# The output offset of the attention: from a matmul ahead of the out projection to an addition on GpSimd

## What is computed

```python
def xattn(Q, K, V, Wq, bq, Wk, bk, Wv, bv, We, be):
    q, k, v = heads(Q @ Wq + bq), heads(K @ Wk + bk), heads(V @ Wv + bv)   # 16 heads of 16
    A = softmax(scale * q @ k.T)                                           # 64 keys
    return merge(A @ v) @ We + be

x = x + xattn(layernorm(x), ctx, ctx, ...)
x = x + ffn(layernorm(x), ...)       # router: the best 2 of 8 experts of 256 -> 1024 -> 256
```

## Time and profile before

| | before |
|---|---|
| median of 3 runs | 405.82 us (405.77 to 406.33) |
| the profiled execution | 406.0 us, of it 403.5 us span |
| mean granted clock of PE in the profile | 0.988 |
| PE, DVE, ACT, POOL busy | 370.9, 242.4, 180.1, 159.0 us |

### The profile page before, as it was taken

The page is one execution under the profiler, slowest core; times in us unless marked ns, Lnnn a source line. Parts: engine busy times, 40 slices in busy tenths (PEclk is TensorE's granted clock), DMA queues, the critical chain, the costliest instruction groups (busy, mean ns, idle before and its releaser), DMA issues.

```text
span 403.5 us, 8452 instructions
## 1 busy us (share of the span) xinstructions
PE 370.9 (92%) x2521; PEld 326.4 (81%) x2522; DVE 242.4 (60%) x693; ACT 180.1 (45%) x283; POOL 159.0 (39%) x186
## 2 busy tenths in 40 slices
PE   8998988998898888989889999999999999999990
PEld 8775667576566656988889999999999999999990
DVE  4267596789979975878334366574747447342440
ACT  1263544444444424643325557465474274262340
POOL 2043402212040204115454683846648718616522
PEclk9999999999999999998999999999999999999996
DMA  8910301041031111155232373937556522312322
GB/s 271 352 72 1 106 0 53 2 158 54 0 105 54 53 55 54 54 155 162 42 57 26 66 226 78 251 92 202 169 105 210 106 25 53 56 23 45 49 24 26
DMA packets 26389, 37.23 MB, mean 92 GB/s; under 512 B 4705, under 2 KB 17441, under 8 KB 26369
## 3 DMA queue, kind: packets, MB, share of 16 engines
q1 hardware_dynamic: 19312, 26.98, 20.2%
q0 software_dynamic: 7056, 9.99, 14.3%
HBM read 27.18 MB, written 9.79 MB: 92 GB/s over the span
## 4 chain that ended last, share of the span: by engine, by line
PE 73%; DVE 15%; issue 5%; POOL 3%; ACT 3%; DMA 1%; DVEq 0%; POOLq 0%; ACTq 0%
PE bankC L1255 10%; PE bankC L1257 10%; PE bankC L1256 10%; PE bankD L1619 7%; PE bankD L1620 6%; PE bankD L1621 6%; DVE nmax L798 3%; PE bankC L1454 3%; PE bankA L1587 2%; PE bankA L1349 2%; PE bankC L1619 2%; PE bankC L1450 2%; PE bankC L1620 1%; PE bankC L1621 1%; POOL rstd L374 1%
## 5 line engine op out<-in xcount | busy, mean ns | idle before, releaser
L700 ACT ACTIVATE hh<-bankC 128x512 fp32r<-128x512 f32 (+1 forms) x52 | 36.3, 697 | 93.3 <-PE bankC L1257 93.3
L1255 PE MATMUL bankC<-xnT_h,up_w 128*128 128x256 f32 (+1 forms) x240 | 74.5, 310 | 2.0 <-ACT prime L694 1.4
L1256 PE MATMUL bankC<-xnT_l,up_w 128*128 128x256 f32 (+1 forms) x240 | 72.9, 304 | 0.0
L1257 PE MATMUL bankC<-xnT_h,up_w 128*128 128x256 f32 (+1 forms) x240 | 72.8, 303 | 0.0
L1619 PE MATMUL bankD<-dn_w,hh 128*128 x208 | 59.9, 288 | 0.9 <-issue 0.5
L1620 PE MATMUL bankD<-dn_w,hh 128*128 x208 | 58.3, 280 | 0.5 <-issue 0.5
L1621 PE MATMUL bankD<-dn_w,hl 128*128 x208 | 58.1, 279 | 0.0
L450 POOL DMA_INDIRECT xr<-rows,idx_g x35 | 47.3, 1353 | 14.8 <-issue 14.0
L1182 DVE TENSOR_TENSOR hl<-prob,hh 128x512 fp32r<-128x512 f32 (+1 forms) x26 | 21.2, 816 | 46.1 <-ACT prob L701 46.1
L1255 PEld LDWEIGHTS bankC<-xnT_h,up_w 128*128 128x128 f32 x240 | 45.5, 190 | 2.9 <-ACT prime L694 1.6
L1256 PEld LDWEIGHTS bankC<-xnT_l,up_w 128*128 128x128 f32 x240 | 45.7, 191 | 0.0
(11 more groups left out here) (312 smaller groups left out, 866.9 us busy)
## 6 DMA issues: line engine op xcount, KB each, us to landing
xall<-up SPq DMA_DIRECT2D x24, 256.0 KB, 3.8
xall<-down SPq DMA_DIRECT2D x24, 256.0 KB, 4.2
rows<-xr SPq DMA_DIRECT2D x4, 528.0 KB, 3.3
raw<-up SPq DMA_DIRECT2D x4, 512.0 KB, 4.7
raw<-down SPq DMA_DIRECT2D x4, 512.0 KB, 5.3
out<-xall SPq DMA_DIRECT2D x4, 512.0 KB, 2.8
xall<-x SPq DMA_DIRECT2D x1, 1536.0 KB, 8.2
cst<-const SPq DMA_DIRECT2D x1, 640.0 KB, 8.2
```

What stands on the lines that cost most here:

```text
L700: a.activation(hT_h[:, 2 * q:2 * q + 2, 0:n * P], bank, ACT.Gelu)
L1255: mm(out_, left_h, right_h, start=first, stop=False)
L1256: mm(out_, left_h, right_l, start=False, stop=False)
L1257: return mm(out_, left_l, right_h, start=False, stop=last)
```

## The change

`be` is loaded to all 128 partitions. The two bias matmuls of `project_out` and all that made their operand are gone; the first matmul of each half bank starts the sum. POOL adds be to the four tiles of batch b in `xall` in one instruction, once the first norm of batch b has read them, at the start of turn b + 1 (for the last batch behind the loop). DVE waits for that ahead of the residual.

```diff
-        be_b = sb("be_b", [64, D])
-        be_r = sb("be_r", [P, D], F32R)
+        be_b = sb("be_b", [P, D])
...
+            def bias_added(b):
+
+                pool.wait_ge(v_xn, LT * b + LT)
+                rows_b = xall[:, b * LT:(b + 1) * LT, :]
+                g.tensor_tensor(rows_b, rows_b, be_b[:, :].rearrange("p (a n) -> p a n", a=1).broadcast_to([P, LT, D]),
+                                ALU.add).then_inc(g_be, 1)
+
             for i in range(1, B):
+                bias_added(i - 1)
                 key_blocks(i)
                 halves_rstd2(i - 1)
                 value_blocks(i)
+            bias_added(B - 1)
             pool.wait_ge(v_se, 1)
...
-            a.activation(be_r[0:64, :], be_b[:, :], ACT.Identity).then_inc(a_be, 1)
...
-            v.memset(be_r[64:P, :].bitcast(F32), 0.0).then_inc(v_one, 1)
...
                     dve.wait_ge(p_proj, 2 * b + n + 1)
+                    dve.wait_ge(g_be, b + 1)
                     xs = xall[:, bass.ds(b * LT + 2 * n, 2), :]
...
-            dve.wait_ge(a_be, 1)
-            v.tensor_tensor(be_r[32:64, :], be_b[32:64, :], be_r[32:64, :].bitcast(F32), ALU.subtract)\
-                .then_inc(v_be, 1)
...
             def project_out(b):
-                pe.wait_ge(v_be, 1)
-                pe.wait_ge(v_one, 4)
+                pe.wait_ge(v_one, 3)
                 pe.wait_ge(v_at, KD * b + KD)
-                bias_2 = be_r[:, :].rearrange("p (a n) -> p a n", a=1).broadcast_to([P, 2, D])
                 for n in range(2):
-                    mm(bankB[n][:, :], one_r[:, :], bias_2, start=True, stop=False, skip_group_check=True)
...
-                            mm(out_, at_h[:, k, o], we_h[:, k, :], start=False, stop=False, skip_group_check=True)
+                            mm(out_, at_h[:, k, o], we_h[:, k, :], start=(k == 0), stop=False, skip_group_check=True)
```

More of the change, by code:

```diff
@@ L278, in build @@
             sem(n) for n in "g_zero g_kbd g_vbd g_rstd1 g_rstd2 g_rw g_pack v_one v_w01".split())
-        g_gi, g_si, a_be, v_be, g_vb = (
-            sem(n) for n in "g_gi g_si a_be v_be g_vb".split())
+        g_gi, g_si, g_be, g_vb = (
+            sem(n) for n in "g_gi g_si g_be g_vb".split())
         p_kv, p_xT, p_q, p_s, p_nmT, p_sT, p_av, p_denT = (
@@ L315, in _ @@
             sp.dma_start(bv_b[:, :], bv.rearrange("(a n) -> a n", a=1).broadcast_to([P, D])).then_inc(d_w, 16)
-            sp.dma_start(be_b[:, :], be.rearrange("(a n) -> a n", a=1).broadcast_to([64, D])).then_inc(d_w, 16)
+            sp.dma_start(be_b[:, :], be.rearrange("(a n) -> a n", a=1).broadcast_to([P, D])).then_inc(d_w, 16)
             sp.dma_start(rb[:, :], router_b.rearrange("(a n) -> a n", a=1).broadcast_to([P, NE])).then_inc(d_w, 16)
```

## The result

| | before | after |
|---|---|---|
| median of 4 runs (us) | 405.97 (405.77 to 406.33) | 416.15 (415.32 to 417.28) |
| profiled execution, time / span (us) | 406.0 / 403.5 | 417.28 / 415.5 |
| mean granted clock of TensorE | 0.988 | 0.962 |

The ratio is 1.0242, with an interval of 1.0205 to 1.028: slower, as forecast, but by 10.2 us where the forecast had 5.5, and 2.1 us above the upper end of the range.

A forecast was written before the change was run, and what follows sets the result against it. The attention's chain was taken to change hands between PE, POOL and DVE; DVE stalls of 6.2 us less a 0.7 us gain, on 406.0 us and 0.2 less for the median, gave 411.3 us, range 408.6 to 414.0.

The forecast's parts named there:

- The removed matmuls: Out projections: 0.48 us of PE time less in each of four, 0.7 us of it gained on the path.
- Turns 2 and 3: Out projections of loop turns 2 and 3: DVE is late there, not PE, so the removal gains 0.
- C: Loop turn 2, hot and put around 102 us: batch 2's addition delays the first hot by 2.1 us, all counting.
- Batch 3's 0.2 us: Last batch's out projection: the removal gains between 0 and 0.48 us, taken as 0.2.
- The hold on DVE: POOL's addition holds a DVE instruction beside it until it ends: 2.0, 2.1 and 2.1 us, 6.2 in all.
- A: First norm of batch 1 at 40 us: batch 0's addition delays its first tile, for which PE waits, by 2.0 us.
- Rivals 2 and 3: 2: DVE held only in part, 407.1 or 409.3 us, chance 0.10; 3: DVE keeps the port, 405.1 us, chance 0.08.
- Rival 4: Batch 1's last norm tile doesn't slip in before batch 1's addition: 1.5 us more, 412.8 us; chance 0.06.
- rival 1: Stalls also lower TensorE's clock, 1.65 us a fall: 413.0 us with one, 416.3 with three; chance 0.14.
- the fall at 183: Behind the last batch's slots, before the change: clock at half for some 3.3 us; if it vanishes, 409.7 us.
- D: Loop turn 3, puts from 136.25 us: batch 3's addition delays the first hot by 2.1 us.
- Nothing behind gives this back: Expert stage: it starts from the last batch's table and is PE's own, so it moves as a whole.

The follow-up runs named there:

- e1: The changed kernel without POOL's additions and DVE's wait for them, be left out of the sum; 410.2 us, with more expert work in it.
- e4: The changed kernel with the same four additions moved behind the key blocks, where DVE works from PSUM; 408.47 us, ratio 1.0035.
- e7: e4 with two 512-column products of zeros on PE ahead of the norm's turn in turns 2 and 3; 407.86 us, ratio 1.0031.
- e8: e7 with one more product of zeros ahead of each of the four first-half slots in turns 2 and 3; 405.57 us, ratio 0.9992.
- e3: The changed kernel with each POOL addition cut into four of 128x256 at the same place; 413.48 us, ratio 1.0194.
- e2: The changed kernel with nine matmuls of zeros on PE in each of its three gaps, DVE's stalls kept; 412.88 us, ratio 1.0184.

## Why the prediction was right or wrong

**The removed matmuls.** In turn 1 0.48 us was forecast and 0.47 seen. Turns 2 and 3 were put at 0; DVE does set the end there, but the step didn't ask what the wide matmuls were as work for PE ahead of a thin stretch. e1 and e4 have a fall of the clock there with no stall at all, so the removal may cost as well. That is not shown: with as many columns put back (e7) a fall stays at C, and only filling the stretch itself (e8) takes it away. Batch 3's 0.2 us isn't to be seen: the delay is 12.92 at its residual and 12.88 at its logits.

**The addition's size and place.** 2.3 us forecast, 2.34 to 2.41 measured, in the idle stretches named. The estimate of 2.25 us from the Trainium skill (GPSIMD Engine Reference, section 3.1) lies 4 to 7% under the trace.

**The hold on DVE.** Forecast 2.0, 2.1 and 2.1 us; measured 1.94, 2.10 and 2.09. e3 shows the mechanism: the hold is one POOL instruction long, whatever that length is. e4 shows that it hangs on what DVE runs beside it, not on the addition. At A, where the order was open, POOL's addition starts at 39.82 and DVE's norm at 39.95, and POOL wins. That agrees with the Trainium skill (SBUF — State Buffer, "Who interferes with whom"): the engine that issues first holds the shared pair for its whole instruction. Rivals 2 and 3 fall with this. Rival 4 as well: the delay goes from 3.04 at the turned maxima to 3.00 us at batch 0's logits.

**The step that failed: rival 1, its chance and its price.** The forecast's sum let a stalled PE cost only its wait. The clock stood beside it at 0.14, on the ground that the stretch of 100 to 106 us kept 1.00 before. But that row shows PE busy 4.85 of 6 us, and a stall of 2 us takes away what kept it so; the row was no evidence for the changed stretch. e2 settles it: with stalls and no falls the delay at batch 3's residual is 5.4 us (5.9 from the first norm tile), with falls 12.9. The price was mis-sized too. It came from the one fall in the trace, 3.3 us long and worth 1.65. A cost 1.57 and fits; C cost 2.2 and D 3.5 us (with the fall at 163), since there the clock was down for 7 and 10 us. Rival 1 with three falls stood at 416.3, near the measured 416.15. Its mechanism is the one that ran, but that its number fits is luck: it had 4.95 us of falls where the ledger has 7.3, and the rest is made up by 0.9 us back for the fall at 183 and by the difference between span and median.

**"Nothing behind gives this back"** held but for that 0.9 us.

What stays open: which single run gets how many falls, why equal waits were followed by 3, 7 and 10 us of half clock, and whether a thin stretch without a long wait falls for what was taken from it or for when it comes. Before itself ran from 404.86 to 409.61 us in these comparisons, and the profiled execution of after was its slowest of four.

## What to carry to other kernels

An addition on an idle engine is free only where no instruction beside it is held by it; look in the trace for instructions that run beside that engine's work and whose twins are shorter, and place the work where there are none. When a change makes TensorE wait, or takes work from it in a thin stretch, count the clock into the sum and not as a side case; a product of zeros in the gap tells the wait's cost from the clock's. The cover that a "useless" matmul gives can be part of what it is worth. And read positions between two traces from a common start: here they differed by up to 0.6 us before the change came in.

## What the runs showed of the hardware

- The clock fell without a long gap. In e4 the granted clock was 0.66 at 103 us, behind slots with gaps of 0.15 us, and 0.50 at 109; with products of zeros in those gaps (e8) it kept 1.00.
- Equal waits were followed by unequal falls: 3 us at half clock behind A, 7 and 10 us behind C and D, each after a wait of 2.2 us. Behind a wait of 0.67 us (e3, at A) there was none.
- A held instruction shows up as a long one, not as a wait: DVE's hot reads 2.36 us busy, so DVE's busy time rose by 5.5 us with two instructions fewer.
- POOL isn't slowed by the DVE instructions that slip in: four additions of 128x256 took 2.82 us beside them, 0.70 each, against 0.73 for one.
